# A threshold search on VectorE and ScalarE: part up to the threshold, a padding column, fewer pointer scalars

## The chip, the cores and the metric

One NeuronCore of a Trainium2 chip runs the whole program. Its engines are TensorE (PE; PEld is its weight load), VectorE (DVE), ScalarE (ACT), GpSimd (POOL) and SyncE (SP), each with an in-order queue; they wait for one another, and for DMAs, by semaphores. The metric is the device time of one execution in microseconds, given as the median of several runs; one further execution was profiled.

## The reference

Two graph layers over 3327 nodes with 256 features each, both with a residual and a layer norm in front. Nearly all of the change lies in the first one, which in each of two steps keeps, in every row of an attention matrix, the largest entries whose softmax mass reaches 0.9, and normalizes them again:

```python
def _adj_from_feats(Xa, W1, W2, W3):
    logits = (Xa @ W1) @ W2 @ (Xa @ W3).T / TAU
    idx = jnp.argsort(-logits, axis=1)
    vals = jnp.take_along_axis(logits, idx, axis=1)
    csum = jnp.cumsum(jax.nn.softmax(vals, axis=1), axis=1)
    k_i = jnp.sum(csum < P_NUC, axis=1) + 1          # P_NUC = 0.9
    keep_sorted = jnp.arange(logits.shape[1])[None, :] < k_i[:, None]
    keep = jnp.take_along_axis(keep_sorted, jnp.argsort(idx, axis=1), axis=1)
    return jax.nn.softmax(jnp.where(keep, logits, -jnp.inf), axis=1)

for s in range(2):
    A = _adj_from_feats(Xa, W1, W2, W3)
    Xf, Xb, Xa = Rf @ Xf, Rb @ Xb, A @ Xa
    Z = Z + (Xf @ U1[s] + Xb @ U2[s] + Xa @ U3[s])
```

The second layer is a masked softmax over x W (x W)^T with an edge mask, and a product with it.

## The kernel before, in words

The rows of the attention matrix are cut into 26 row tiles of 128 partitions; a row tile is 128 x 3327 in float32 (`rows`, six buffers of `NPAD` = 3328 columns, of which the last is zeroed once). Nothing is sorted. The exponentials x of a row are kept, with their sum Z, and a threshold `mid` is searched by 19 rounds of bisection on a logarithmic scale (`BISECT` = 19): each round asks whether the entries above `mid` hold 0.9 Z, and multiplies `mid` by one of two constants, `up` or `down` (`rate`). After 19 rounds `cut` zeroes what lies at or below `mid`, and its sum is the new normalizer.

`layer_step` is one of the two steps. Its row tiles run in nine triples g = 0 to 8. In triples 0 to 7 all three roles run side by side: VectorE searches the row tiles r = 0 and r = 1, ScalarE r = 2. This document calls such a triple a block. The last one, `LAST` = 8, has two row tiles: VectorE does r = 0 alone, ScalarE the first 10 rounds of r = 1 (`FIRST_PART`), then VectorE takes r = 1 over (`take_over`, `go_on`).

A round on VectorE is three instructions. `evaluate` (L720; `alone` L741 and `go_on` L758 in the last triple) is a pass over the row tile that sums x where x > `mid`; the accumulator read that ends it is an instruction of its own in the trace. `judge` (L727, L761) compares the sum with `target` = 0.9 Z, both on one column, and writes `hit`. `move` (L732, L764) sets `mid` = (`hit` + `down`) * `mid`. In a block the two row tiles alternate, one slot each, 38 slots in all: pass of r, `move` of the other one, `judge` of r, then `between`. `between` puts other work of VectorE into the slots by a table of beats (`due`): `take` (L699) evicts a 512-wide chunk of the next block's logits from PSUM, `highest` (L705) reduces their maxima, `cut` (L774), `scale`, `row_sums`, `row_rates`, `low_parts`. In the last triple each of the three waits for the one before.

A round on ScalarE has two passes over its row tile: Sign (L673), which counts, and Relu (L679), which sums what is above the threshold; `mid` is kept negated as a bias. `sides` prepares `base`, `fac` and `mean` from `mid`, `above` forms `over` from the count, `settle` the sign and the new `mid`. Between the passes and after the second, `fill` does ScalarE's other work by beats 0 to 39, two a round: it evacuates transposed weights from PSUM (`evacuate`, L552), for TensorE's products (`attend`), and outputs, issues DMAs, and takes the next block's three exponentials (L517) at beats 20, 29 and 37. TensorE's queue holds, beat by beat, the next logits (two PSUM banks, freed by `take`), transposes, `attend` and the sweeps of other products.

After the two steps come two phases, a middle one and one over the edges of the second layer.

Of the kernel before, what the change touches and what calls it, by code (L numbers as in the profile page):

```python
# [7 lines left out]
ALU = mybir.AluOpType  # L8
# [7 lines left out]
P = 128  # L16
# [323 lines left out]
def layer_step(nc, sem_in, psum, sb_in, s, qk, s_op, a_op, env):  # L340
# [40 lines left out]
    with ExitStack() as c:  # L381
        sb = sb_in(c)
        sem, cleared = sem_in(c)
        rows = sb(tag + "rows", [P, 6, NPAD], F32)
        dump = sb(tag + "dump", [P, N], BF16)
        adump = sb(tag + "adump", [P, N], I8)
# [6 lines left out]
            sb(tag + n, [P, 6], F32) for n in ("nb", "Z", "target", "mid", "hit", "mass", "kept", "rk"))  # L393
        cnt, gap, base, over, sgn, fac, mean = (sb(tag + n, [P, 1], F32) for n in ("cnt", "gap", "base", "over", "sgn", "fac", "mean"))
        u12 = sb(tag + "u12", [P, KC, 2 * D], F32)
        S = {n: sem(tag + n) for n in (
            "lg_done", "lg_free", "nb_ready", "exp_done", "w_ready", "rk_ready", "tr_done", "ev_done", "ax_done",
            "acc_free", "slab_used", "sa_free", "rows_zero", "a_eval", "a_begun", "a_base", "a_over", "a_sgn", "a_fac", "a_mid",
            "weights")}
# [31 lines left out]
        def row(g, r):  # L431
            return rows[:, home(g, r), 0:N]

        def w2d(ap):
# [78 lines left out]
        def _(act):  # L513
# [6 lines left out]
            def begin(g, r):  # L520
                act.wait_ge(S["exp_done"], LOADS.index((g, r)) + 1)
                nc.scalar.activation(st(target, g, 2), st(Z, g, r), ACT.Copy, scale=2.0 * P_NUC).then_inc(S["a_begun"], 1)
                nc.scalar.activation(st(mid, g, 2), st(Z, g, r), ACT.Copy, scale=-LEAST * 2.0 ** LOG_STEP).then_inc(S["a_begun"], 1)
                act.wait_ge(S["a_begun"], 2 * (g + 1))

            def sides(g, it):
                up, down = rate(it)
                last = -1.0 if it + 1 == BISECT else 1.0
                nc.scalar.activation(base[:], st(mid, g, 2), ACT.Identity, scale=float(N), bias=st(target, g, 2)).then_inc(S["a_base"], 1)
                nc.scalar.activation(fac[:], st(mid, g, 2), ACT.Copy, scale=last * (down - up) / 2).then_inc(S["a_fac"], 1)  # L530
                nc.scalar.activation(mean[:], st(mid, g, 2), ACT.Copy, scale=last * (down + up) / 2).then_inc(S["a_fac"], 1)

            def above(g, n):
                act.wait_ge(S["a_base"], n + 1)
                act.wait_ge(S["a_eval"], 2 * n + 1)
                nc.scalar.activation(over[:], cnt[:], ACT.Identity, scale=st(mid, g, 2), bias=base[:]).then_inc(S["a_over"], 1)

            def settle(g, n):
                act.wait_ge(S["a_over"], n + 1)
                act.wait_ge(S["a_eval"], 2 * n + 2)  # L540
                nc.scalar.activation(sgn[:], gap[:], ACT.Sign, scale=-2.0, bias=over[:]).then_inc(S["a_sgn"], 1)
                act.wait_ge(S["a_sgn"], n + 1)
                act.wait_ge(S["a_fac"], 2 * n + 2)
                nc.scalar.activation(st(mid, g, 2), sgn[:], ACT.Identity, scale=fac[:], bias=mean[:]).then_inc(S["a_mid"], 1)
                act.wait_ge(S["a_mid"], n + 1)

# [121 lines left out]
            for g in range(TRIPLES):  # L668
                r, rounds = (1, FIRST_PART) if g == LAST else (2, BISECT)
                begin(g, r)  # L670
                for it in range(rounds):
                    n = BISECT * g + it
                    nc.scalar.activation(adump[:], row(g, r), ACT.Sign, bias=st(mid, g, 2), accum_out=cnt[:]).then_inc(S["a_eval"], 1)  # L673
                    sides(g, it)
                    for b in beats(g, 2 * it):
                        fill(g, b)
                    above(g, n)
                    act.wait_ge(S["a_eval"], 2 * n + 1)
                    nc.scalar.activation(adump[:], row(g, r), ACT.Relu, bias=st(mid, g, 2), accum_out=gap[:]).then_inc(S["a_eval"], 1)  # L679
                    for b in beats(g, 2 * it + 1):  # L680
                        fill(g, b)
                    settle(g, n)
            for b in range(2 * FIRST_PART + NGRP + 4, 2 * BISECT):
# [6 lines left out]
        def _(dve):  # L690
# [16 lines left out]
            def begin(g, r):  # L707
                dve.wait_ge(S["exp_done"], LOADS.index((g, r)) + 1)
                nc.vector.tensor_scalar(st(target, g, r), st(Z, g, r), P_NUC, None, ALU.mult).then_inc(begun[r], 1)
                nc.vector.tensor_scalar(st(mid, g, r), st(Z, g, r), LEAST * 2.0 ** LOG_STEP, None, ALU.mult).then_inc(begun[r], 1)  # L710

            def evaluate(g, it, r):
                n = BISECT * g + it
                if it == 0:
                    dve.wait_ge(begun[r], 2 * (g + 1))
                else:
                    dve.wait_ge(mid_ready[r], n)
                if n + r >= 1:
                    dve.wait_ge(mass_done[1 - r], n + r)
                nc.vector.scalar_tensor_tensor(out=dump[:], in0=row(g, r), scalar=st(mid, g, r), in1=row(g, r),  # L720
                                               op0=ALU.is_gt, op1=ALU.mult, accum_out=st(mass, g, r)).then_inc(mass_done[r], 1)

            def judge(g, it, r):
                n = BISECT * g + it
                up, down = rate(it)
                dve.wait_ge(mass_done[r], n + 1)
                nc.vector.tensor_scalar(st(hit, g, r), st(mass, g, r), st(target, g, r), up - down, ALU.is_ge, ALU.mult).then_inc(hit_ready[r], 1)  # L727

            def move(g, it, r):
                n = BISECT * g + it  # L730
                dve.wait_ge(hit_ready[r], n + 1)
                nc.vector.tensor_scalar(st(mid, g, r), st(hit, g, r), rate(it)[1], st(mid, g, r), ALU.add, ALU.mult).then_inc(mid_ready[r], 1)  # L732

            def alone(it):
                n = BISECT * LAST + it
                if it == 0:
                    dve.wait_ge(begun[0], 2 * (LAST + 1))
                    dve.wait_ge(mass_done[1], n)
                else:
                    dve.wait_ge(mid_ready[0], n)  # L740
                nc.vector.scalar_tensor_tensor(out=dump[:], in0=row(LAST, 0), scalar=st(mid, LAST, 0), in1=row(LAST, 0),  # L741
                                               op0=ALU.is_gt, op1=ALU.mult, accum_out=st(mass, LAST, 0)).then_inc(mass_done[0], 1)
                judge(LAST, it, 0)
                move(LAST, it, 0)

            def take_over():
                dve.wait_ge(S["a_mid"], BISECT * LAST + FIRST_PART)
                nc.vector.tensor_scalar(st(target, LAST, 1), st(Z, LAST, 1), P_NUC, None, ALU.mult).then_inc(begun[1], 1)
                nc.vector.tensor_scalar(st(mid, LAST, 1), st(mid, LAST, 2), -1.0, None, ALU.mult).then_inc(mid_ready[1], 1)

            def go_on(it):
                n = BISECT * LAST + it - FIRST_PART
                up, down = rate(it)
                if it == FIRST_PART:
                    dve.wait_ge(begun[1], 2 * LAST + 1)
                    dve.wait_ge(mass_done[0], BISECT * TRIPLES)
                dve.wait_ge(mid_ready[1], n + 1)
                nc.vector.scalar_tensor_tensor(out=dump[:], in0=row(LAST, 1), scalar=st(mid, LAST, 1), in1=row(LAST, 1),  # L758
                                               op0=ALU.is_gt, op1=ALU.mult, accum_out=st(mass, LAST, 1)).then_inc(mass_done[1], 1)
                dve.wait_ge(mass_done[1], n + 1)  # L760
                nc.vector.tensor_scalar(st(hit, LAST, 1), st(mass, LAST, 1), st(target, LAST, 1), up - down,  # L761
                                        ALU.is_ge, ALU.mult).then_inc(hit_ready[1], 1)
                dve.wait_ge(hit_ready[1], n + 1)
                nc.vector.tensor_scalar(st(mid, LAST, 1), st(hit, LAST, 1), down, st(mid, LAST, 1), ALU.add, ALU.mult).then_inc(mid_ready[1], 1)  # L764

            def cut(g, r):
# [5 lines left out]
                else:  # L772
                    dve.wait_ge(mid_ready[r], BISECT * (g + 1))
                nc.vector.scalar_tensor_tensor(out=row(g, r), in0=row(g, r), scalar=st(mid, g, r), in1=row(g, r),  # L774
                                               op0=ALU.is_gt, op1=ALU.mult,
# [77 lines left out]
            for g in range(LAST):  # L853
                begin(g, 0)
                for it in range(BISECT):
                    for r in range(2):
# [3 lines left out]
                        if it + r >= 1:  # L860
                            move(g, it + r - 1, 1 - r)
                        judge(g, it, r)
                        between(g, 2 * it + r)
                cut(g, 0)
# [749 lines left out]
```

## Time and profile before

| | before |
|---|---|
| median of 3 runs | 3754.25 us (3752.21 to 3756.71) |
| profiled execution, own time | 3752.47 us |
| its span, first to last instruction | 3750.6 us |
| busy share DVE / ACT / PE / PEld / POOL | 94% / 84% / 78% / 55% / 10% |
| granted TensorE clock, mean | 0.892 |

The shares are of the whole span. A stretch's own busy times say which engine is full in it; the time of an instruction overlaps that of the next on the same engine, so two rows of the timeline are read by their starts. The idle time that a row names, and what ended it, belong to the engine in front of that instruction.

### The profile page before, as it was taken

How to read it: one execution, taken by the hardware profiler on the slowest of the kernel's cores; microseconds unless marked ns; L12 is line 12 of the kernel's file. 1: busy time of each engine (PE TensorE's matmuls, PEld its weight loads, DVE VectorE, ACT ScalarE, POOL GpSimd, SP SyncE). 2: the span in 40 equal slices, each digit the busy share in tenths (PEclk: the TensorE clock that was granted, in tenths of full speed). 3: DMA queues.
4: the chain of work that ended last, by engine and by line, in shares of the span. 5: the costliest groups of instructions: out<-in, count | busy, mean ns of one | idle time of the engine just before them, and what ended most of it. 6: DMA issues, size and time to landing. Idle time of an engine off the chain costs nothing. (4 is left out here: it accounts for less than half of the span.)

```text
span 3750.6 us, 42354 instructions
## 1 busy us (share of the span) xinstructions
PE 2934.6 (78%) x14004; PEld 2072.7 (55%) x14004; DVE 3507.9 (94%) x4688; ACT 3148.4 (84%) x4587; POOL 387.2 (10%) x457
## 2 busy tenths in 40 slices
PE   6568787787878788538879797978889754799998
PEld 4456666675757566413536354544536343567787
DVE  7999999999999999789999999999999995677887
ACT  6999999999999999479899999999999971344443
POOL 3000000000000000000000000000000002334444
PEclk9689888898989898769989898989999877999999
DMA  2112121312222220072121121212121103355563
GB/s 93 64 56 87 62 92 59 104 46 94 67 74 83 75 79 22 27 206 65 33 51 37 42 50 35 50 39 44 42 53 38 31 6 99 104 170 189 197 210 106
DMA packets 157020, 288.52 MB, mean 77 GB/s; under 512 B 14080, under 2 KB 93376, under 8 KB 153408
## 3 DMA queue, kind: packets, MB, share of 16 engines
q1 hardware_dynamic: 120400, 205.97, 17.7%
q10 hardware_dynamic: 21744, 62.79, 4.8%
q0 software_dynamic: 14656, 17.04, 3.3%
q8 instruction: 111, 1.82, 0.2%
q14 instruction: 109, 0.89, 0.1%
HBM read 232.80 MB, written 59.77 MB: 78 GB/s over the span
## 5 line engine op out<-in xcount | busy, mean ns | idle before, releaser
L720 DVE SCALAR_TENSOR_TENSOR s_dump<-s_rows,s_mid 128x3327 bf16<-128x3327 f32 x608 | 2238.5, 3682 | 2.3 <-issue 0.7
L673 ACT ACTIVATE s_adump<-s_rows,s_mid 128x3327 int8<-128x3327 f32 x324 | 995.1, 3071 | 10.5
L679 ACT ACTIVATE s_adump<-s_rows,s_mid 128x3327 int8<-128x3327 f32 x324 | 991.0, 3059 | 0.0
L932 PE MATMUL bank<-x,s_slab 128*128 128x512 f32 x1352 | 633.7, 612 | 0.0
L909 PE MATMUL bank<-kh,qs 128*128 128x512 f16 (+1 forms) x364 | 147.0, 404 | 379.6 <-DVE s_rows L699 369.5
L932 PEld LDWEIGHTS bank<-x,s_slab 128*128 128x128 f32 x1352 | 266.3, 198 | 280.3 <-issue 268.4
L976 PE MATMUL bank<-hb,s_wT 128*128 128x256 f32 x1352 | 358.4, 410 | 72.5 <-ACT s_wT L552 72.4
L976 PE MATMUL bank<-xab,s_wT 128*128 128x256 f32 x1352 | 349.1, 403 | 49.9 <-ACT s_wT L552 49.8
L965 PE MATMUL bank<-ident,s_rows 128*128 128x128 f32 x1352 | 231.3, 299 | 183.9 <-DVE s_rows L774 183.0
L932 PE MATMUL bank<-hb,s_slab 128*128 128x257 f32 x1352 | 351.0, 400 | 0.0
L976 PEld LDWEIGHTS bank<-hb,s_wT 128*128 128x128 f32 x1352 | 262.8, 205 | 123.1 <-ACT s_wT L552 55.9
L965 PEld LDWEIGHTS bank<-ident,s_rows 128*128 128x128 f32 x1352 | 188.5, 157 | 250.4 <-DVE s_rows L774 191.3
L976 PEld LDWEIGHTS bank<-xab,s_wT 128*128 128x128 f32 x1352 | 258.5, 202 | 93.0 <-ACT s_wT L552 42.3
L552 ACT ACTIVATE s_wT<-bank 128x512 f32<-128x512 f32 (+1 forms) x364 | 199.6, 550 | 127.9 <-PE bank L965 127.6
L909 PEld LDWEIGHTS bank<-kh,qs 128*128 128x128 f16 x364 | 42.9, 118 | 476.4 <-DVE s_rows L699 445.2
L932 PEld LDWEIGHTS bank<-hb,s_slab 128*128 128x128 f32 x1352 | 269.8, 202 | 60.2 <-issue 17.9
L1414 ACT ACTIVATE e_wh<-bank 128x512 f16<-128x512 f32 (+1 forms) x182 | 101.2, 565 | 202.0 <-PE bank L1546 201.6
L699 DVE TENSOR_SCALAR_CACHE_REDUCE s_rows<-bank 128x512 f32<-128x512 f32 (+1 forms) x364 | 232.7, 643 | 4.8 <-PE bank L910 3.4
L1363 POOL TENSOR_TENSOR e_rows<-e_rows,e_adj 128x3328 f32<-128x3328 f32 x25 | 181.2, 7247 | 233.2 <-ACT e_rows L1375 233.2
L937 PEld LDWEIGHTS bank<-hb,strip 128*128 128x128 f32 x1352 | 190.4, 197 | 13.2
L774 DVE SCALAR_TENSOR_TENSOR s_rows<-s_rows,s_mid 128x3327 f32<-128x3327 f32 x52 | 191.4, 3680 | 0.9
L494 POOL COPY qs<-s_q 64x128 f16<-64x128 f16 x26 | 32.5, 1249 | 1516.6 <-ACT s_q L618 1516.6
(183 smaller groups left out, 4824.2 us busy)
## 6 DMA issues: line engine op xcount, KB each, us to landing
s_slab<-adjT_dram SPq DMA_DIRECT2D x104, 448.0 KB, 3.9
s_slab<-adjT_dram SPq DMA_DIRECT2D x104, 384.0 KB, 3.7
e_adj<-adjR_dram ACTq DMA_DIRECT2D x23, 1664.0 KB, 7.2
strip<-adjR_dram SPq DMA_DIRECT2D x52, 448.0 KB, 3.5
strip<-adjR_dram SPq DMA_DIRECT2D x52, 384.0 KB, 3.3
e_ring<-sc_d SPq DMA_DIRECT2D x72, 256.0 KB, 5.4
sc_d<-e_stage SPq DMA_DIRECT2D x60, 256.0 KB, 2.4
su_d<-s_su_out ACTq DMA_DIRECT2D x26, 256.0 KB, 2.0
```

The source lines that it names most:

```text
L552: nc.scalar.activation(wT[:, n % 2, 0:w], bank_of("quad", n)[:, 0:w], ACT.Copy).then_inc(S["ev_done"], 1)
L673: nc.scalar.activation(adump[:], row(g, r), ACT.Sign, bias=st(mid, g, 2), accum_out=cnt[:]).then_inc(S["a_eval"], 1)
L679: nc.scalar.activation(adump[:], row(g, r), ACT.Relu, bias=st(mid, g, 2), accum_out=gap[:]).then_inc(S["a_eval"], 1)
L699: nc.vector.tensor_scalar(rows[:, home(g, r), ch * CH:ch * CH + w], psL[n % 2][:, 0:w], 1.0, None, ALU.mult, ALU.max, accum_out=mx[:, home ...
L720: nc.vector.scalar_tensor_tensor(out=dump[:], in0=row(g, r), scalar=st(mid, g, r), in1=row(g, r), op0=ALU.is_gt, op1=ALU.mult, accum_out=s ...
L774: nc.vector.scalar_tensor_tensor(out=row(g, r), in0=row(g, r), scalar=st(mid, g, r), in1=row(g, r), op0=ALU.is_gt, op1=ALU.mult, accum_out ...
L909: nc.tensor.matmul(psL[n % 2][:, 0:w], lhs, kh2[:, cols], start=True, stop=False)
L932: ins = nc.tensor.matmul(acc, slab[:, i % NSLAB, j - PIECES[p], :], s_op[:, j, 0:SN], start=False, stop=(j == NT - 1))
L937: ins = nc.tensor.matmul(psS[t % 2][:, SN + j:SN + j + 1], strip[:, i % 2, k * P:(k + 1) * P], s_op[:, 0, D:SN], start=False, stop=(j == N ...
L965: ins = nc.tensor.transpose(bank[:, k * P:(k + 1) * P], rows[:, home(g, r), j * P:(j + 1) * P], ident[:])
L976: ins = nc.tensor.matmul(psA[f % 2][:, 0:D], wT[:, n % 2, k * P:(k + 1) * P], a_op[:, j, 0:D], start=(j == 0), stop=(j == NT - 1))
L1363: nc.gpsimd.tensor_tensor(em[:, t % 3], em[:, t % 3], adj[:, t % 3], ALU.mult).then_inc(S["w_ready"], 1)
```

## The change

On VectorE the pass sums x where x <= `mid` instead of x > `mid`. It covers all 3328 columns (`wide_row`); `begin` writes (0.9 - 1) Z into the last one (`rest`) in place of `target`, so the sum is that of the entries up to `mid` less 0.1 Z, and `judge` compares it with the constant 0. `judge` then has two constants as scalars; `move` becomes a scalar_tensor_tensor with a constant as its scalar and `mid` as its second stream. `cut` covers the wide row too. `between` stands ahead of `judge`.

On ScalarE the second pass is Abs instead of Relu: with the sum of |x - t| and the count, `base` isn't needed, and its instruction goes. `target` becomes (2 * 0.9 - 1) Z. `above` and the second pass follow the first one directly; the even beat's `fill` moves behind the second pass, the odd one's behind `settle`. The wait for the new `mid` moves from the end of `settle` to the start of the next round.

```diff
-        dump = sb(tag + "dump", [P, N], BF16)
+        dump = sb(tag + "dump", [P, NPAD], BF16)
...
+        def wide_row(g, r):
+            return rows[:, home(g, r), :]
+
+        def rest(g, r):
+            return rows[:, home(g, r), N:NPAD]
...
             def sides(g, it):
...
-                nc.scalar.activation(base[:], st(mid, g, 2), ACT.Identity, scale=float(N), bias=st(target, g, 2)).then_inc(S["a_base"], 1)
...
             def above(g, n):
-                act.wait_ge(S["a_base"], n + 1)
                 act.wait_ge(S["a_eval"], 2 * n + 1)
-                nc.scalar.activation(over[:], cnt[:], ACT.Identity, scale=st(mid, g, 2), bias=base[:]).then_inc(S["a_over"], 1)
+                nc.scalar.activation(over[:], cnt[:], ACT.Identity, scale=st(mid, g, 2), bias=st(target, g, 2)).then_inc(S["a_over"], 1)
...
-                nc.scalar.activation(sgn[:], gap[:], ACT.Sign, scale=-2.0, bias=over[:]).then_inc(S["a_sgn"], 1)
+                nc.scalar.activation(sgn[:], gap[:], ACT.Sign, scale=-1.0, bias=over[:]).then_inc(S["a_sgn"], 1)
...
-                act.wait_ge(S["a_mid"], n + 1)
...
+                    if it >= 1:
+                        act.wait_ge(S["a_mid"], n)
                     nc.scalar.activation(adump[:], row(g, r), ACT.Sign, bias=st(mid, g, 2), accum_out=cnt[:]).then_inc(S["a_eval"], 1)
                     sides(g, it)
+                    above(g, n)
+                    nc.scalar.activation(adump[:], row(g, r), ACT.Abs, bias=st(mid, g, 2), accum_out=gap[:]).then_inc(S["a_eval"], 1)
                     for b in beats(g, 2 * it):
                         fill(g, b)
-                    above(g, n)
-                    act.wait_ge(S["a_eval"], 2 * n + 1)
-                    nc.scalar.activation(adump[:], row(g, r), ACT.Relu, bias=st(mid, g, 2), accum_out=gap[:]).then_inc(S["a_eval"], 1)
+                    settle(g, n)
                     for b in beats(g, 2 * it + 1):
                         fill(g, b)
-                    settle(g, n)
...
             def begin(g, r):
                 dve.wait_ge(S["exp_done"], LOADS.index((g, r)) + 1)
-                nc.vector.tensor_scalar(st(target, g, r), st(Z, g, r), P_NUC, None, ALU.mult).then_inc(begun[r], 1)
+                nc.vector.tensor_scalar(rest(g, r), st(Z, g, r), P_NUC - 1.0, None, ALU.mult).then_inc(begun[r], 1)
...
-                nc.vector.scalar_tensor_tensor(out=dump[:], in0=row(g, r), scalar=st(mid, g, r), in1=row(g, r),
-                                               op0=ALU.is_gt, op1=ALU.mult, accum_out=st(mass, g, r)).then_inc(mass_done[r], 1)
+                nc.vector.scalar_tensor_tensor(out=dump[:], in0=wide_row(g, r), scalar=st(mid, g, r), in1=wide_row(g, r),
+                                               op0=ALU.is_le, op1=ALU.mult, accum_out=st(mass, g, r)).then_inc(mass_done[r], 1)
...
-                nc.vector.tensor_scalar(st(hit, g, r), st(mass, g, r), st(target, g, r), up - down, ALU.is_ge, ALU.mult).then_inc(hit_ready[r], 1)
+                nc.vector.tensor_scalar(st(hit, g, r), st(mass, g, r), 0.0, up - down, ALU.is_le, ALU.mult).then_inc(hit_ready[r], 1)
...
-                nc.vector.tensor_scalar(st(mid, g, r), st(hit, g, r), rate(it)[1], st(mid, g, r), ALU.add, ALU.mult).then_inc(mid_ready[r], 1)
+                nc.vector.scalar_tensor_tensor(out=st(mid, g, r), in0=st(hit, g, r), scalar=rate(it)[1], in1=st(mid, g, r),
+                                               op0=ALU.add, op1=ALU.mult).then_inc(mid_ready[r], 1)
...
                         evaluate(g, it, r)
                         if it + r >= 1:
                             move(g, it + r - 1, 1 - r)
+                        between(g, 2 * it + r)
                         judge(g, it, r)
-                        between(g, 2 * it + r)
```

`alone`, `go_on`, `take_over` and `cut` are changed in the same way.

## Rows read from the trace of the kernel before

**Rows 1.** Stretches: length, busy us (instructions) of PE, PEld, DVE, ACT, POOL; clock, DMA.
```profile
581.90:754.80 172.90, 137.84 (x684) 110.92 (x684) 172.46 (x221) 168.34 (x247) 4.21 (x3) 0.88 0.24 76
3115.10:3750.60 635.50, 552.28 (x4198) 443.71 (x4198) 462.10 (x839) 266.61 (x432) 255.89 (x237) 0.96 0.49 159
```

**Rows 2.** VectorE's groups by line and shape: count, busy us, mean ns, idle before.
```profile
L720 DVE SCALAR_TENSOR_TENSOR s_dump<-s_rows,s_mid 128x3327 bf16<-128x3327 f32 x608 | 2238.5, 3682 | 2.3 <-issue 0.7
...
L732 DVE TENSOR_SCALAR s_mid<-s_hit,s_mid 128x1 f32<-128x1 f32 x646 | 135.2, 209 | 1.3
L727 DVE TENSOR_SCALAR s_hit<-s_mass,s_target 128x1 f32<-128x1 f32 x646 | 133.8, 207 | 1.9
...
L1187 DVE SCALAR_TENSOR_TENSOR m_x<-m_tin,m_inv 128x256 f32<-128x256 f32 x26 | 11.4, 478 | 0.0
...
L710 DVE TENSOR_SCALAR s_mid<-s_Z 128x1 f32<-128x1 f32 x34 | 4.9, 144 | 0.0
...
L1492 DVE TENSOR_TENSOR e_rows<-e_rows,e_adj 128x3328 f32<-128x3328 f32 x1 | 3.6, 3627 | 2.3 <-ACT e_rows L1375 2.3
```

**Rows 3.** Timeline of VectorE, steady slots: start us, length us, engine, line.
```profile
712.00 0.21 DVE L732 TENSOR_SCALAR s_mid<-s_hit,s_mid 128x1 f32<-128x1 f32 x1
712.13 0.21 DVE L727 TENSOR_SCALAR s_hit<-s_mass,s_target 128x1 f32<-128x1 f32 x1
712.25 0.68 DVE L699 TENSOR_SCALAR_CACHE_REDUCE s_rows<-bank 128x512 f32<-128x512 f32 x1
...
716.47 0.21 DVE L732 TENSOR_SCALAR s_mid<-s_hit,s_mid 128x1 f32<-128x1 f32 x1
716.59 0.21 DVE L727 TENSOR_SCALAR s_hit<-s_mass,s_target 128x1 f32<-128x1 f32 x1
716.72 3.68 DVE L720 SCALAR_TENSOR_TENSOR s_dump<-s_rows,s_mid 128x3327 bf16<-128x3327 f32 x1
```

**Rows 4.** Timeline of VectorE where a block begins.
```profile
758.61 0.08 DVE L720 DVE_READ_ACCUMULATOR s_dump<-s_rows,s_mid 128x1 f32 x1
758.72 0.21 DVE L727 TENSOR_SCALAR s_hit<-s_mass,s_target 128x1 f32<-128x1 f32 x1
758.85 0.14 DVE L709 TENSOR_SCALAR s_target<-s_Z 128x1 f32<-128x1 f32 x1
758.91 0.14 DVE L710 TENSOR_SCALAR s_mid<-s_Z 128x1 f32<-128x1 f32 x1
759.09 3.69 DVE L720 SCALAR_TENSOR_TENSOR s_dump<-s_rows,s_mid 128x3327 bf16<-128x3327 f32 x1
```

**Rows 5.** Timeline of VectorE in the last triple of step 1.
```profile
2988.93 0.21 DVE L727 TENSOR_SCALAR s_hit<-s_mass,s_target 128x1 f32<-128x1 f32 x1
2989.18 0.21 DVE L732 TENSOR_SCALAR s_mid<-s_hit,s_mid 128x1 f32<-128x1 f32 x1
2989.43 3.69 DVE L741 SCALAR_TENSOR_TENSOR s_dump<-s_rows,s_mid 128x3327 bf16<-128x3327 f32 x1
```

**Rows 6.** ScalarE: three groups by line, then two rows of its timeline.
```profile
L679 ACT ACTIVATE s_adump<-s_rows,s_mid 128x3327 int8<-128x3327 f32 x324 | 991.0, 3059 | 0.0
...
L529 ACT ACTIVATE s_base<-s_mid,s_target 128x1 f32<-128x1 f32 x324 | 90.5, 279 | 0.0
...
L265 ACT ACT_TABLE_LOAD x1 | 1.3, 1283 | 0.7 <-PEq L1607 0.7
...
732.77 0.28 ACT L529 ACTIVATE s_base<-s_mid,s_target 128x1 f32<-128x1 f32 x1
732.95 0.19 ACT L530 ACTIVATE s_fac<-s_mid 128x1 f32<-128x1 f32 x1
```

**Rows 7.** Timeline of ScalarE: the third exponential for the block that begins at 754.75.
```profile
745.39 3.06 ACT L517 ACTIVATE s_rows<-s_rows,s_nb 128x3327 f32<-128x3327 f32 x1
```

**Rows 8.** Timeline of VectorE: the take-over in step 0, with idle time before.
```profile
1531.49 0.15 DVE L748 TENSOR_SCALAR s_target<-s_Z 128x1 f32<-128x1 f32 x1 [0.97 <-ACT s_mid L544]
```

**Rows 9.** Waits from 409 to 1273 us: total us, times, longest us.
```profile
PE bank L909 <- DVE s_rows L699: 91.2, 36, 6.0
```

More of the change, by code:

```diff
@@ L393, in layer_step @@
             sb(tag + n, [P, 6], F32) for n in ("nb", "Z", "target", "mid", "hit", "mass", "kept", "rk"))
-        cnt, gap, base, over, sgn, fac, mean = (sb(tag + n, [P, 1], F32) for n in ("cnt", "gap", "base", "over", "sgn", "fac", "mean"))
+        cnt, gap, over, sgn, fac, mean = (sb(tag + n, [P, 1], F32) for n in ("cnt", "gap", "over", "sgn", "fac", "mean"))
         u12 = sb(tag + "u12", [P, KC, 2 * D], F32)
@@ L397, in layer_step @@
             "lg_done", "lg_free", "nb_ready", "exp_done", "w_ready", "rk_ready", "tr_done", "ev_done", "ax_done",
-            "acc_free", "slab_used", "sa_free", "rows_zero", "a_eval", "a_begun", "a_base", "a_over", "a_sgn", "a_fac", "a_mid",
+            "acc_free", "slab_used", "sa_free", "rows_zero", "a_eval", "a_begun", "a_over", "a_sgn", "a_fac", "a_mid",
             "weights")}
@@ L521, in begin @@
                 act.wait_ge(S["exp_done"], LOADS.index((g, r)) + 1)
-                nc.scalar.activation(st(target, g, 2), st(Z, g, r), ACT.Copy, scale=2.0 * P_NUC).then_inc(S["a_begun"], 1)
+                nc.scalar.activation(st(target, g, 2), st(Z, g, r), ACT.Copy, scale=2.0 * P_NUC - 1.0).then_inc(S["a_begun"], 1)
                 nc.scalar.activation(st(mid, g, 2), st(Z, g, r), ACT.Copy, scale=-LEAST * 2.0 ** LOG_STEP).then_inc(S["a_begun"], 1)
@@ L740, in alone @@
                     dve.wait_ge(mid_ready[0], n)
-                nc.vector.scalar_tensor_tensor(out=dump[:], in0=row(LAST, 0), scalar=st(mid, LAST, 0), in1=row(LAST, 0),
-                                               op0=ALU.is_gt, op1=ALU.mult, accum_out=st(mass, LAST, 0)).then_inc(mass_done[0], 1)
+                nc.vector.scalar_tensor_tensor(out=dump[:], in0=wide_row(LAST, 0), scalar=st(mid, LAST, 0), in1=wide_row(LAST, 0),
+                                               op0=ALU.is_le, op1=ALU.mult, accum_out=st(mass, LAST, 0)).then_inc(mass_done[0], 1)
                 judge(LAST, it, 0)
@@ L747, in take_over @@
                 dve.wait_ge(S["a_mid"], BISECT * LAST + FIRST_PART)
-                nc.vector.tensor_scalar(st(target, LAST, 1), st(Z, LAST, 1), P_NUC, None, ALU.mult).then_inc(begun[1], 1)
+                nc.vector.tensor_scalar(rest(LAST, 1), st(Z, LAST, 1), P_NUC - 1.0, None, ALU.mult).then_inc(begun[1], 1)
                 nc.vector.tensor_scalar(st(mid, LAST, 1), st(mid, LAST, 2), -1.0, None, ALU.mult).then_inc(mid_ready[1], 1)
@@ L757, in go_on @@
                 dve.wait_ge(mid_ready[1], n + 1)
-                nc.vector.scalar_tensor_tensor(out=dump[:], in0=row(LAST, 1), scalar=st(mid, LAST, 1), in1=row(LAST, 1),
-                                               op0=ALU.is_gt, op1=ALU.mult, accum_out=st(mass, LAST, 1)).then_inc(mass_done[1], 1)
+                nc.vector.scalar_tensor_tensor(out=dump[:], in0=wide_row(LAST, 1), scalar=st(mid, LAST, 1), in1=wide_row(LAST, 1),
+                                               op0=ALU.is_le, op1=ALU.mult, accum_out=st(mass, LAST, 1)).then_inc(mass_done[1], 1)
                 dve.wait_ge(mass_done[1], n + 1)
-                nc.vector.tensor_scalar(st(hit, LAST, 1), st(mass, LAST, 1), st(target, LAST, 1), up - down,
-                                        ALU.is_ge, ALU.mult).then_inc(hit_ready[1], 1)
+                nc.vector.tensor_scalar(st(hit, LAST, 1), st(mass, LAST, 1), 0.0, up - down, ALU.is_le, ALU.mult).then_inc(hit_ready[1], 1)
                 dve.wait_ge(hit_ready[1], n + 1)
-                nc.vector.tensor_scalar(st(mid, LAST, 1), st(hit, LAST, 1), down, st(mid, LAST, 1), ALU.add, ALU.mult).then_inc(mid_ready[1], 1)
+                nc.vector.scalar_tensor_tensor(out=st(mid, LAST, 1), in0=st(hit, LAST, 1), scalar=down, in1=st(mid, LAST, 1),
+                                               op0=ALU.add, op1=ALU.mult).then_inc(mid_ready[1], 1)
             def cut(g, r):
@@ L773, in cut @@
                     dve.wait_ge(mid_ready[r], BISECT * (g + 1))
-                nc.vector.scalar_tensor_tensor(out=row(g, r), in0=row(g, r), scalar=st(mid, g, r), in1=row(g, r),
+                nc.vector.scalar_tensor_tensor(out=wide_row(g, r), in0=wide_row(g, r), scalar=st(mid, g, r), in1=wide_row(g, r),
                                                op0=ALU.is_gt, op1=ALU.mult,
```

## The prediction

> **What bounds the kernel now.** The first view to read is the busy time by stretch. From 582 to 755 us, one block of three row tiles of the search, VectorE is busy 172.46 of 172.90 us, while ScalarE has about 4.6 us to spare and TensorE 35; the last 635.5 us belong to phases that the diff doesn't touch [rows 1]. There are 16 such blocks (eight in each of two layer steps), and two short ones that end a step. So VectorE's chain of instructions sets the time of the search, 16 x 172.9 us = 2766 us and the two short blocks, and what it sheds there the kernel sheds, until ScalarE or TensorE comes late. The second view is the groups by line: a search pass costs 3682 ns, and each of 646 rounds also has a `judge` (207 ns) and a `move` (209 ns) on one column [rows 2]. The third is the timeline, because durations overlap: what counts is the distance from one start to the next. In a slot with an eviction, `move` starts at 712.00, `judge` at 712.13, the eviction at 712.25. In a slot with nothing between, `move` starts at 716.47, `judge` at 716.59 and the next pass at 716.72 [rows 3]. Either small instruction thus holds VectorE for 0.125 us, 0.25 us together, and ends some 82 ns after its follower began.
>
> **`judge` without a pointer.** Where both scalars are constants, one column takes 0.14 us, and the next instruction starts 0.06 us later (758.85 to 758.91) [rows 4]. I take 0.062 instead of 0.125 us. One limit stays: what reads a pass's sum starts 0.11 to 0.12 us after the accumulator read (758.61 to 758.72) [rows 4]. The old `move` filled that time; a shorter one leaves part of it open.
>
> **`move` as scalar_tensor_tensor with a constant.** This form is not in the trace. With a pointer, the form costs 3682 ns at 3327 columns and 478 at 256 [rows 2]: 1.043 ns a column and 212 ns for a single one. A tensor_tensor, also two streams and without a pointer, takes 3627 ns at 3328 columns [rows 2], so some 156 for one. Taking the price of a pointer (207 against 144, 64 ns) off 212 gives 148. I take 152, near both, and so 0.070 us of engine time. The ends are 144 (as cheap as the constant-only form: 0.062) and 212 (the constant saves nothing: 0.130). Below or above these I see no reason. Something that waits for its result starts 0.04 us after its end: a constant-only writer is followed at 0.18 (758.91 to 759.09), a pointer one at 0.25 (2989.18 to 2989.43) [rows 4, 5]. For the new `move` that is 0.19 us (ends 0.18 and 0.25).
>
> The Trainium skill's VectorE: DVE Perf Modes, section "The TRN2 errata", gives an SBUF instruction 58 cycles plus its columns at 0.96 GHz, whatever its scalars; worked out from it, an estimate of 61 ns for one column, and nothing to gain: the kernel would stay at 3753 us, against 3685 by the rows. The rows at 0.125 against 0.06 us speak against that for pointers, and agree for constants [rows 3, 4].
>
> **The sum, by slots.** By `between`'s beats the 16 blocks of 38 slots have 401 with work between (evictions, maxima, cuts, low parts), 175 without, 16 first slots (no `move`), and 16 last ones, with a cut behind.
> - With work between: before 0.25. After, `move` 0.070, the work, then `judge` 0.062; the sum has long been there, which is what the new order of `between` and `judge` is good for. 0.118 each, 401 times: 47.3 us.
> - Without work, and last slots: the next pass waits for the `move` in front of the `judge`, 0.19 us after its start; `judge` (start at 0.12, held 0.062) ends at about the same time. 0.25 becomes 0.19: 0.060, 191 times: 11.5 us.
> - First slots: `judge` alone, 0.063, 16 times: 1.0 us. The `move` ahead of a block's second cut: 0.055, 16 times: 0.9 us.
> - The two short blocks run one row tile at a time, 19 + 9 rounds each: pass, `judge`, `move`, each waiting for the one before at 0.25 us (2988.93, 2989.18, 2989.43) [rows 5]. The two become 0.18 and 0.19: 0.128, 56 times: 7.2 us.
> - Against it: the wide pass and the wide cut have one column more, 1.04 ns, on 664 passes and 52 cuts: 0.7 us. `begin` and `take_over` issue as many instructions as before.
>
> Together 67.9 less 0.7 is 67.2 us. With the cheapest `move` it is 72.9, with the dearest 27.4.
>
> **ScalarE.** The round loses the base instruction: 279 ns long, 0.18 us to the next start (732.77 to 732.95) [rows 6]. 19 of them are 3.5 us a block, 60 us in all, none on the path as long as VectorE bounds. VectorE sheds about (67.2 - 7.2) / 16 = 3.8 us a block, so ScalarE must not lose more than its 4.6 us of idle and the missing 0.3 us. The even beats' evacuations go behind the second pass, where they cover the wait for its sum; the odd ones go behind the new threshold and cover part of that wait, where they covered the other one before. I cost this between 0 and 1 us a block, in either direction. Cover stays: the third exponential starts at 745.39 and lasts 3.06 us [rows 7], and the row tile that needs it first begins at 758.85 [rows 4], ten microseconds after. A lag of 0.5 us a block over eight blocks would fit in. Where the cover is thin is the end of step 0: VectorE waits 0.97 us for ScalarE's tenth round [rows 8]. There VectorE sheds 19 x 0.128 = 2.4 us and ScalarE 10 x 0.18 = 1.8, so this wait may be 0 to 2 us instead of 1. I cost it at no change.
>
> **What is moved.** The even evacuations come later by a pass (3059 ns long [rows 6]), and TensorE's products behind them too. Its queue holds the next logits behind these products, and VectorE's evictions wait for the logits. TensorE has two banks of lead: in five blocks it waited 91.2 us in 36 waits, up to 6.0 us, for evictions to free them [rows 9]. A shift of 3 us fits. ScalarE's DMA issues move with their beats; the stores they make are needed in the next step only. SP's queue loads slabs as TensorE's sweeps free them; these slip by the same 3 us, with two or three slabs loaded ahead. POOL adds ScalarE's outputs in DRAM, and ScalarE needs their buffers again a row tile later, a third of a block.
>
> So the forecast is 3752.47 us (the profiled execution's own time, 1.9 us more than its span) less 67.2, **3685.3 us**, say 3685. The runs' median, 3754.25, lies 1.8 us above this profile; the range holds that.
>
> **Rivals.**
> - The constant in the two-stream form saves nothing: `move` keeps its price, 27.4 us are saved, 3725 us. For it: no row has the form. Against it: tensor_tensor, at 156, has two streams and no pointer [rows 2]. Chance 0.06.
> - The waits in empty slots don't bind, and all 191 save 0.118: 11 us more, 3674 us. Against it: 0.18 and 0.25 behind a writer [rows 4, 5]. Chance 0.04.
> - The small instructions' start-to-start time is the sequencer's and not the pointer's, so that nothing is saved: 3752.5 + 0.7 = 3753 us. Against it: 0.06 against 0.125 in neighbouring rows [rows 4]. Chance 0.03. (This is what the errata section quoted above comes to.)
> - Slower, by TensorE: its lead is less than the pass by which the even evacuations slip. Then in the two even beats that have both an evacuation and an eviction (10 and 12), logits come 3.3 us late: 2 x 3.3 x 16 = 106 us lost, 3752.5 - 67.2 + 106 = 3791 us. It decides from a lead under about 3 us; the waits of up to 6.0 us speak against it [rows 9]. Chance 0.03.
> - Slower, by ScalarE: Abs is not in the function table that is loaded once, 1283 ns, in the whole span [rows 6]. Then each round switches twice, 19 x 2 x 1.283 = 48.8 us a block; ScalarE, with 172.9 - 4.6 - 3.5 = 164.8 of its own, needs 213.6 where a block lasted 172.9: 40.7 us more, 16 times, some 4400 us. It decides as soon as switching costs over 4 us a block. Exp, Sign, Relu, Identity and Copy share the one load, which says nothing of Abs. Chance 0.02.
>
> The Trainium skill's ScalarE: Activation LUTs, section "Table sets", says that abs is filler in every set; by that no load is added and this last rival falls. No run here has shown it.
>
> **How the numbers follow.** The forecast has 0.80; 0.02 is left for a ScalarE that falls behind by more than its cover, within some 20 us. About 0.2%, 7.5 us, is what a measurement of this kernel can tell from no change. Faster: 0.80 + 0.06 + 0.04 + 0.02 = 0.92; same 0.03; slower 0.05. The range runs from 3673 (empty slots save in full) to 3712 (a `move` of some 190 ns, or a ScalarE that is late by 20 us and more).
>
> **What would show it.** `judge` falls from 207 to about 145 ns and `move` from 209 to about 152. In an empty slot the distance from accumulator read to next pass falls from 0.25 to 0.19; with an eviction, `move` is followed at 0.07. A block falls from 172.9 to about 169 us, with VectorE still idle for well under 1 us in it and ScalarE idle for some microseconds. There is one table load. The forecast is wrong if idle time of VectorE appears ahead of evictions, exponentials' readers or the first cut of a block, or if `move` is at 209 or above.

## The result and the profile after

| | before | after |
|---|---|---|
| median | 3753.57 us (4 runs) | 3730.95 us (4 runs, 3729.09 to 3731.34) |
| ratio | 1 | 0.9937, 95% interval 0.9923 to 0.9952 |
| profiled execution, its span | 3752.47, 3750.6 us | 3731.06, 3729.3 us |
| busy DVE, whole span | 3507.9 us | 3446.5 us |

The change saves 22.6 us, a third of the 67.2 that were forecast, and the time lies outside the range (3673 to 3712). VectorE's busy time fell by 61.4 us, so most of the forecast work did go; 40 us of it came back as idle time. The stretches tell where. Each row has the columns of [rows 1]; the first is a block, the next two run from the begin of the last triple to its last cut, in step 0 and step 1, and the two behind them are the same stretches of the kernel before:

```profile
572.50:741.80 169.30, 139.15 (x684) 110.97 (x684) 168.81 (x219) 161.96 (x228) 1.80 (x3) 0.89 0.24 78
1415.20:1564.20 149.00, 98.39 (x392) 73.14 (x392) 123.92 (x139) 91.41 (x143) 3.52 (x4) 0.81 0.05 18
2954.10:3090.30 136.20, 69.59 (x304) 57.54 (x304) 120.15 (x127) 81.22 (x115) 5.11 (x6) 0.76 0.06 6
```
```profile
1441.80:1573.10 131.30, 90.72 (x391) 67.39 (x389) 127.05 (x139) 93.88 (x151) 4.19 (x4) 0.84 0.06 21
2985.00:3111.30 126.30, 61.81 (x301) 51.60 (x299) 123.19 (x126) 85.11 (x127) 5.11 (x6) 0.77 0.06 7
```

The block is down from 172.90 to 169.30 us with VectorE full, as argued; ScalarE has 7.3 us to spare in it instead of 4.6 [rows 1]. The last triples, 131.3 and 126.3 us long before, have grown to 149.0 and 136.2, and VectorE is idle in them for 25.1 and 16.1 us, where it was for 4.3 and 3.1. From the first begin to the last triple's, the eight blocks went from 1371.7 to 1344.3 us in step 0 and from 1363.3 to 1340.8 in step 1: -27.4 and -22.5, while VectorE's busy time in them fell by 27.4 and 28.1. With +17.7 and +9.9 in the last triples that is -22.3 of the span's -21.3. What comes after the last cut of a step is as long as before, within a microsecond.

VectorE's groups of the two small instructions, which answer to [rows 2]:

```profile
L736 DVE SCALAR_TENSOR_TENSOR s_mid<-s_hit,s_mid 128x1 f32<-128x1 f32 x646 | 101.4, 157 | 1.3
L731 DVE TENSOR_SCALAR s_hit<-s_mass 128x1 f32<-128x1 f32 x646 | 96.8, 150 | 2.5
```

`judge` is down from 207 to 150 ns, `move` from 209 to 157, close to the 145 and 152 that were said. The wide pass costs nothing that shows (3679 ns on average against 3682). The timeline of an empty slot and of one with an eviction, as [rows 3]:

```profile
627.91 0.15 DVE L736 SCALAR_TENSOR_TENSOR s_mid<-s_hit,s_mid 128x1 f32<-128x1 f32 x1
628.02 0.15 DVE L731 TENSOR_SCALAR s_hit<-s_mass 128x1 f32<-128x1 f32 x1
628.10 3.69 DVE L724 SCALAR_TENSOR_TENSOR s_dump<-s_rows,s_mid 128x3328 bf16<-128x3328 f32 x1
...
631.71 0.16 DVE L736 SCALAR_TENSOR_TENSOR s_mid<-s_hit,s_mid 128x1 f32<-128x1 f32 x1
631.78 0.69 DVE L703 TENSOR_SCALAR_CACHE_REDUCE s_rows<-bank 128x512 f32<-128x512 f32 x1
...
632.39 0.15 DVE L731 TENSOR_SCALAR s_hit<-s_mass 128x1 f32<-128x1 f32 x1
632.46 3.68 DVE L724 SCALAR_TENSOR_TENSOR s_dump<-s_rows,s_mid 128x3328 bf16<-128x3328 f32 x1
```

The empty slot spends 0.19 us on the two (627.91 to 628.10), the other one 0.07 and 0.07. Both are the forecast's.

What VectorE waits for now, in total us, times, longest us, and behind it `low_parts` in the kernel before:

```profile
DVE kl L803 <- ACT s_q L621: 38.8, 3, 23.7
...
DVE s_rows L753 <- ACT s_mid L548: 19.8, 2, 12.9
...
DVE s_rows L703 <- PE bank L915: 8.9, 18, 2.5
```
```profile
DVE kl L798 <- ACT s_q L618: 23.4, 1, 23.4
```

The take-over (L753) waits 19.8 us for ScalarE's tenth round; before, it waited 0.97 us in step 0 [rows 8] and nothing in step 1. `low_parts` (L803) waits 15.1 us in the last triple of step 0; before, its one wait, 23.4 us, lay behind the last cut of that step, and a wait as long (23.7) lies there still. Evictions (L703) wait 8.9 us for logits against 3.4; the 5.4 us that are new lie in the blocks of step 1, and none in those of step 0. The first two are the last triples.

ScalarE's timeline at the start of the last triple of step 0 shows why:

```profile
1416.30 0.57 ACT L555 ACTIVATE s_wT<-bank 128x512 f32<-128x512 f32 x1
1416.77 0.28 ACT L545 ACTIVATE s_sgn<-s_gap,s_over 128x1 f32<-128x1 f32 x1
1417.09 0.39 ACT L548 ACTIVATE s_mid<-s_sgn,s_mean,s_fac 128x1 f32<-128x1 f32 x1
1417.38 0.57 ACT L555 ACTIVATE s_wT<-bank 128x512 f32<-128x512 f32 x1
1421.60 0.60 ACT L555 ACTIVATE s_wT<-bank 128x512 f32<-128x512 f32 x1 [3.64 <-PE bank L970]
...
1428.99 1.08 ACT L555 ACTIVATE s_wT<-bank 128x512 f32<-128x512 f32 x2
1429.95 0.31 ACT L545 ACTIVATE s_sgn<-s_gap,s_over 128x1 f32<-128x1 f32 x1
1430.29 0.39 ACT L548 ACTIVATE s_mid<-s_sgn,s_mean,s_fac 128x1 f32<-128x1 f32 x1
1434.31 0.60 ACT L555 ACTIVATE s_wT<-bank 128x512 f32<-128x512 f32 x1 [3.64 <-PE bank L970]
1436.69 0.38 ACT L555 ACTIVATE s_wT<-bank 128x256 f32<-128x256 f32 x1 [1.78 <-PE bank L970]
```

In the last triple `beats` gives each half of a round two beats, hence two evacuations in the first rounds, where a block has one. Before, a pass stood between one pair and the next, and TensorE did its products meanwhile. Now both pairs come one after the other (1428.99, then 1434.31 and 1436.69), with only the two small settling instructions between. There are two `wT` buffers and two banks, so the third evacuation has to wait until TensorE has used the first and transposed the next piece (up to four 128 x 128 tiles) into its bank, and ScalarE stands still. Then it runs two passes in a row, and TensorE stands still. ScalarE's evacuations in its ten rounds of step 0 and step 1, with the idle time before them and what ended most of it, the first two now, the next two in the kernel before:

```profile
L555 ACT ACTIVATE s_wT<-bank 128x512 f32<-128x512 f32 (+1 forms) x21 | 11.3, 558 | 22.4 <-PE bank L970 22.4
L555 ACT ACTIVATE s_wT<-bank 128x512 f32<-128x512 f32 (+1 forms) x22 | 11.9, 558 | 21.1 <-PE bank L970 21.1
```
```profile
L552 ACT ACTIVATE s_wT<-bank 128x512 f32<-128x512 f32 (+1 forms) x21 | 11.2, 553 | 3.3 <-PE bank L965 3.2
L552 ACT ACTIVATE s_wT<-bank 128x512 f32<-128x512 f32 (+1 forms) x21 | 11.2, 553 | 7.5 <-PE bank L965 7.4
```

### The profile page after: what moved, and what is told of

Same layout as the page of the kernel before. It is cut to its first block and busy times, and to the rows that moved or that the text cites. A ratio compares the mean times of both kernels' runs of the same rounds, so it can differ in the third digit from the quotient of the medians.

```text
span 3729.3 us, 41687 instructions
## 1 busy us (share of the span) xinstructions
PE 2935.2 (79%) x14004; PEld 2079.7 (56%) x14004; DVE 3446.5 (92%) x4688; ACT 3067.7 (82%) x4263; POOL 387.3 (10%) x457
## 3 DMA queue, kind: packets, MB, share of 16 engines
q1 hardware_dynamic: 120400, 205.97, 17.7%
## 5 line engine op out<-in xcount | busy, mean ns | idle before, releaser
L724 DVE SCALAR_TENSOR_TENSOR s_dump<-s_rows,s_mid 128x3328 bf16<-128x3328 f32 x608 | 2236.8, 3679 | 2.1 <-issue 0.9
L937 PE MATMUL bank<-x,s_slab 128*128 128x512 f32 x1352 | 624.5, 605 | 0.0
L981 PE MATMUL bank<-xab,s_wT 128*128 128x256 f32 x1352 | 360.7, 413 | 89.1 <-ACT s_wT L555 88.8
L981 PEld LDWEIGHTS bank<-xab,s_wT 128*128 128x128 f32 x1352 | 266.0, 207 | 136.5 <-ACT s_wT L555 60.4
L703 DVE TENSOR_SCALAR_CACHE_REDUCE s_rows<-bank 128x512 f32<-128x512 f32 (+1 forms) x364 | 233.8, 646 | 10.4 <-PE bank L915 8.9
L779 DVE SCALAR_TENSOR_TENSOR s_rows<-s_rows,s_mid 128x3328 f32<-128x3328 f32 x52 | 191.4, 3682 | 0.7
```

The source lines that it names most:

```text
L703: nc.vector.tensor_scalar(rows[:, home(g, r), ch * CH:ch * CH + w], psL[n % 2][:, 0:w], 1.0, None, ALU.mult, ALU.max, accum_out=mx[:, home ...
L724: nc.vector.scalar_tensor_tensor(out=dump[:], in0=wide_row(g, r), scalar=st(mid, g, r), in1=wide_row(g, r), op0=ALU.is_le, op1=ALU.mult, a ...
L779: nc.vector.scalar_tensor_tensor(out=wide_row(g, r), in0=wide_row(g, r), scalar=st(mid, g, r), in1=wide_row(g, r), op0=ALU.is_gt, op1=ALU. ...
L937: ins = nc.tensor.matmul(acc, slab[:, i % NSLAB, j - PIECES[p], :], s_op[:, j, 0:SN], start=False, stop=(j == NT - 1))
L981: ins = nc.tensor.matmul(psA[f % 2][:, 0:D], wT[:, n % 2, k * P:(k + 1) * P], a_op[:, j, 0:D], start=(j == 0), stop=(j == NT - 1))
```

## The experiments

Seven kernels. The times are medians of four runs each (ten for the row of four), the ratios against the kernel before on the same chip (3754.73 us for the first four, 3754.09 for the others).

**The last triple back to its old places.** The changed kernel, with ScalarE's other work where it was, for the last triple alone:

```diff
                     sides(g, it)
+                    early = g == LAST
+                    if early:
+                        for b in beats(g, 2 * it):
+                            fill(g, b)
                     above(g, n)
                     nc.scalar.activation(adump[:], row(g, r), ACT.Abs, ...)
-                    for b in beats(g, 2 * it):
+                    for b in beats(g, 2 * it + 1 if early else 2 * it):
                         fill(g, b)
                     settle(g, n)
-                    for b in beats(g, 2 * it + 1):
-                        fill(g, b)
+                    if not early:
+                        for b in beats(g, 2 * it + 1):
+                            fill(g, b)
```

> The changed kernel, with the other work of ScalarE put back to its old places in the last triple alone (even beat between the two passes, odd beat between the second pass and the sign); base stays removed. Theory A: in the last triple each half of a round has two evacuations, the new places put four in a row, and the third and fourth wait for TensorE (22.4 and 21.1 us of such waits in the last triple of step 0 and 1, against 3.3 and 7.5 before), which makes VectorE wait at the take-over and at its low parts. Then these waits fall to under 8 us a step, VectorE's stretch from the begin of the last triple to its last cut falls from 149.0 and 136.2 us to about 129 and 124, and the time is some 3699 us. Theory B: the waits come from VectorE reaching the take-over earlier, whatever ScalarE's places: then 3725 us or more.

Measured: 3700.0 us, ratio 0.9855 (0.984 to 0.987), 31 us less than the changed kernel. The two last triples, then ScalarE's evacuations in its ten rounds of each:

```profile
1415.10:1543.30 128.20, 85.58 (x389) 63.55 (x388) 123.94 (x140) 91.43 (x142) 7.01 (x4) 0.86 0.06 21
2935.60:3058.80 123.20, 58.90 (x301) 49.24 (x299) 120.09 (x127) 83.45 (x118) 5.11 (x6) 0.78 0.06 7
```
```profile
L555 ACT ACTIVATE s_wT<-bank 128x512 f32<-128x512 f32 (+1 forms) x21 | 11.3, 555 | 1.8 <-PE bank L975 1.7
L555 ACT ACTIVATE s_wT<-bank 128x512 f32<-128x512 f32 (+1 forms) x21 | 11.2, 555 | 2.4 <-PE bank L975 2.2
```

128.2 and 123.2 us, as theory A has it, and 1.7 and 2.2 us of waits for TensorE instead of 22.4 and 21.1. Theory B falls: VectorE reaches the take-over of step 0 earlier than in the changed kernel, where `low_parts` had held it up, and waits 1.1 us there.

**VectorE's half alone.** ScalarE's code is that of before, `base` included.

> VectorE's half of the change alone: ScalarE has its base instruction, Relu, and the old places. Theory A: the blocks last about 169.3 and 167 us as in the changed kernel, the last triples have few waits on TensorE (3 to 8 us), VectorE waits about 3 us at the take-over of step 0 (0.97 plus 19 x 0.128); 3697 to 3705 us. Theory B: VectorE waits 7 us or more at both take-overs; 3725 us or more. A third possibility: ScalarE with its base instruction is the bound of the blocks; then these last over 170 us and VectorE is idle in them.

Measured: 3702.74 us, ratio 0.9863 (0.9848 to 0.9877). The waits of VectorE in question:

```profile
DVE s_rows L705 <- PE bank L917: 11.9, 20, 2.2
DVE s_rows L755 <- ACT s_mid L550: 5.2, 1, 5.2
```

A single wait at a take-over, as theory A has it, but 5.2 us and not 3. New are 11.9 us of waits for logits, more than in any other kernel, and the blocks of step 1 take 1344.0 us together against 1334.9 with the old places and no base (below). I read this as a trace of the third possibility: with its base instruction ScalarE is slower, TensorE waits for its evacuations, and the logits stand behind those in TensorE's queue. The traces show the middle of it: in the blocks of step 1 TensorE waits 65.0 us for evacuations here and 43.0 us there. That the logits come late for this reason is argued.

**ScalarE's half alone.** VectorE's code is that of before; the moved work and the missing base stay.

> ScalarE's half of the change alone: VectorE has its pointer scalars and the old sum. Theory A: blocks unchanged at 172.7 and 170.4 us, waits on TensorE in the last triples at about 20 us as in the changed kernel, VectorE waits at low parts and the take-over; slower than before by 15 to 30 us, some 3775 us. Theory B: as before within 5 us, 3750 to 3755 us.

Measured: 3779.76 us, ratio 1.0066 (1.0051 to 1.0081): this half makes the kernel slower by 25.0 us. The waits of VectorE, and ScalarE's evacuations in its ten rounds of step 0:

```profile
DVE kl L796 <- ACT s_q L615: 36.2, 2, 23.4
DVE s_target L746 <- ACT s_mid L542: 15.8, 2, 9.0
```
```profile
L549 ACT ACTIVATE s_wT<-bank 128x512 f32<-128x512 f32 (+1 forms) x21 | 11.3, 558 | 22.8 <-PE bank L963 22.8
```

ScalarE's waits are those of the changed kernel (22.8 us against 22.4) without any edit on VectorE: its speed has no part in them. In the blocks the missing base saves nothing, as VectorE sets their length (172.9 us, as before).

**The old places everywhere.** `early = True` in the first experiment's code; base stays removed, Abs stays.

> The changed kernel with the old places of ScalarE's other work in all triples (base removed, Abs). Theory A: the last triples as with the old places there alone; the blocks at 169 and 167 us or a little less, since evacuations are not a pass late and VectorE's waits for logits (8.9 us against 3.4 before) go back; 3690 to 3700 us. If the new places are what keeps ScalarE in pace in the blocks, these grow instead and VectorE waits for exponentials: over 3710 us.

Measured: 3692.46 us, ratio 0.9834 (0.9818 to 0.985), the fastest of all these kernels, 38.5 us faster than the changed one. The last triples last 128.3 and 123.2 us. VectorE's waits for logits:

```profile
DVE s_rows L708 <- PE bank L920: 3.2, 13, 0.7
```

Against the first experiment the last triples are the same, and so are the blocks of step 0 (1344.4 us in both); the other 7.5 us are the blocks of step 1 (1334.9 us against 1342.5), and 6.8 of them the evictions' waits (10.0 us there). So ScalarE's work that comes a pass late does reach VectorE in those blocks too, by way of TensorE's logits, though by little. Against VectorE's half alone, 10.3 us are what the lighter ScalarE round (no base, Abs for Relu) brings once its other work is left in place.

**Judge ahead of the work between.** On the old places everywhere:

```diff
                         if it + r >= 1:
                             move(g, it + r - 1, 1 - r)
-                        between(g, 2 * it + r)
                         judge(g, it, r)
+                        between(g, 2 * it + r)
```

> Against the changed kernel with the old places of ScalarE's work everywhere (3692.5 us): judge ahead of the work between again. If a judge directly behind a 0.072 us move waits for the pass's sum until 0.118 us after the accumulator read, a slot with work between costs 0.118 + 0.066 instead of 0.072 + 0.066 us: 0.046 more, 401 times, 18 us; some 3711 us, blocks about 1.1 us longer. If the sum is there in time and the order is worth nothing: 3691 to 3695 us.

Measured: 3716.09 us, ratio 0.9899 (0.9883 to 0.9916), 23.6 us more. A slot with an eviction:

```profile
636.05 0.15 DVE L741 SCALAR_TENSOR_TENSOR s_mid<-s_hit,s_mid 128x1 f32<-128x1 f32 x1
636.16 0.15 DVE L736 TENSOR_SCALAR s_hit<-s_mass 128x1 f32<-128x1 f32 x1
636.23 0.68 DVE L708 TENSOR_SCALAR_CACHE_REDUCE s_rows<-bank 128x512 f32<-128x512 f32 x1
```

The judge stands 0.11 us behind the move, waiting for the sum, and 0.18 us go by before the eviction starts. With a cheap `move` the order of `between` and `judge` is worth 23.6 us. 18 were expected.

**Four evacuations in a row, but early.** On the old places everywhere; in the last triple both beats of a round stand between the two passes:

```diff
+                    both = g == LAST
+                    for h in (2 * it, 2 * it + 1) if both else (2 * it,):
+                        for b in beats(g, h):
+                            fill(g, b)
                     above(g, n)
                     nc.scalar.activation(adump[:], row(g, r), ACT.Abs, ...)
+                    if not both:
+                        for b in beats(g, 2 * it + 1):
+                            fill(g, b)
                     settle(g, n)
```

> The old places everywhere (3692.5 us), but in the last triple both beats of a round, four evacuations, between the two passes: in a row, yet earlier than before. If it is the row of four that makes ScalarE wait for TensorE, the waits in the last triples are again 15 to 25 us each, VectorE waits at low parts and the take-over, and the time is 3710 to 3735 us. If it is that the work comes a pass later, there are none of these waits, and the time is 3692 us or a little less.

Measured: 3746.36 us, ratio 0.9978 (0.9969 to 0.9988), 53.9 us more, above the range that was expected for the row. ScalarE's evacuations in its ten rounds of step 0 and step 1, and VectorE's wait at the take-overs:

```profile
L555 ACT ACTIVATE s_wT<-bank 128x512 f32<-128x512 f32 (+1 forms) x21 | 11.3, 556 | 24.4 <-PE bank L973 24.3
L555 ACT ACTIVATE s_wT<-bank 128x512 f32<-128x512 f32 (+1 forms) x22 | 11.9, 559 | 30.4 <-PE bank L973 30.4
```
```profile
DVE s_rows L756 <- ACT s_mid L548: 36.2, 2, 23.1
```

A row of four is enough to bring the waits, without any work being late: nothing here is later than with the old places. Whether the lateness adds to them in the changed kernel is not shown. Why the row costs more here than in the changed kernel was not tried; there the two pairs have at least the settling instructions between them.

**Move with its pointer again.** On the old places everywhere, `move` and `go_on` with the old tensor_scalar:

```diff
-                nc.vector.scalar_tensor_tensor(out=st(mid, g, r), in0=st(hit, g, r), scalar=rate(it)[1], in1=st(mid, g, r),
-                                               op0=ALU.add, op1=ALU.mult).then_inc(mid_ready[r], 1)
+                nc.vector.tensor_scalar(st(mid, g, r), st(hit, g, r), rate(it)[1], st(mid, g, r), ALU.add, ALU.mult).then_inc(mid_ready[r], 1)
```

> The old places everywhere (3692.5 us), but move again as tensor_scalar with a pointer; judge with constants. By the slots: 0.054 x 401 + 0.052 x 191 + 0.057 x 56 + 0.06 x 16 = 36 us more, some 3728 us, with move at 209 ns and 0.126 us from start to start. If VectorE's small instructions are partly covered: under 15 us more.

Measured: 3723.85 us, ratio 0.992 (0.9905 to 0.9935), 31.4 us more, where 36 were expected.

```profile
L741 DVE TENSOR_SCALAR s_mid<-s_hit,s_mid 128x1 f32<-128x1 f32 x646 | 135.1, 209 | 1.3
```

The form of one instruction on one column, run 646 times, is worth 0.9% of the kernel. The edit changes the form and the pointer together, so the pointer's own part is not shown here; `judge`, which kept its form, shows it (207 ns with the pointer, 150 without).

## Why the prediction was wrong

- **What bounds the kernel**: right. In the blocks VectorE is full before and after. In step 0 they fell by what VectorE shed (27.4 us), in step 1 by 22.5 of 28.1. (The 16 blocks last 2735.0 us together before; 16 x 172.9 takes the longer ones of step 0 for all.)
- **`judge` and `move`**: right within 5 ns each (150 and 157 ns against 145 and 152). The form that the trace before didn't have lay between the two ends that were given, 144 and 212 ns, and next to the 156 of the tensor_tensor.
- **The sum by slots**: right in its mechanism, 5 us too large. The kernel with the old places everywhere, which has all of VectorE's edits and none of the new waits, saves 62.3 us where 67.2 were said. A slot with work spends 0.07 + 0.07 us, where 0.070 + 0.062 were said, and an empty one 0.19 (627.91 to 628.10 above) to 0.21, where 0.19 was: some 0.01 us more than the terms, over 592 slots. That `judge` must stand behind the work between was right too: 23.6 us.
- **ScalarE in the blocks**: right. It kept pace; its lead was not used up. Removing its base is not free of effect: 10.3 us, where nothing was counted. In the traces VectorE's waits for logits (11.9 and 3.2 us) and at the take-over (5.2 and 1.1 us) differ with it.
- **The end of a step: the step that failed.** "so this wait may be 0 to 2 us instead of 1. I cost it at no change." It was 19.8 us at the two take-overs and 15.1 at `low_parts`. The working counted ScalarE's own instructions (10 x 0.18 us) and not what its moved work waits for. It also took the last triple to be like a block, whereas `beats` doubles the work there: two evacuations a half-round. Four in a row outrun two buffers. The two last triples together came out 27.6 us longer where 7.2 less were forecast: 34.8 us. Undoing the places there alone took 33.8 us out of the two triples and 31.0 off the time, and a row of four put elsewhere brought the waits back. By the spans 45.9 us of the forecast are missing: these 34.8, then 10.1 in the blocks (4.5 that VectorE did not shed, and 5.6 of idle time in step 1), and 1.0 elsewhere.
- **What is moved: "A shift of 3 us fits"**: nearly. It holds in step 0; in the blocks of step 1 evictions wait 5.4 us, where they didn't wait before. With the old places everywhere these are gone (3.2 us of such waits in the whole span, 3.4 before the change), and the kernel is 7.5 us faster than with the last triples mended alone. The rival on TensorE had the mechanism, at far too large a price (106 us): its lead of two banks takes up most of the shift.
- **Rivals**: the dear `move` (3725), the empty slots without a wait (3674) and small instructions that save nothing (3753) fall by the timeline and by the last experiment. A pointer costs 57 ns in `judge`; `move` shed 52 ns with its pointer, but its form changed too. The Trainium skill's VectorE: DVE Perf Modes, section "The TRN2 errata", has a formula without a term for a pointer; the measurement differs and decides. There is one table load, 1283 ns, as before, with Abs among the functions, so the dear Abs falls too. The Trainium skill's ScalarE: Activation LUTs, section "Table sets", has abs in every set; this trace agrees.

The range missed because it had some 20 us for a ScalarE that falls behind in the blocks, but 2 us at most for the wait at the end of a step, without a bound from the rows on TensorE's time between two evacuations. Before, ScalarE already stood up to 1.69 us between the two evacuations of a pair in that triple.

## What to carry to other kernels

When work is moved within an engine's queue, count not only its own instructions. Ask what another engine did for it while the long instruction between two pieces ran. If the pieces are put next to each other and there are more of them than buffers, that other engine's time shows in full. Look for the stretches where the schedule is denser than in the steady state, such as the last group, and cost those by their own rows. And of two halves of a change measure each alone: here one was worth 52 us and the other cost 25.

## What the runs showed of the hardware

TensorE ran slower after it had stood still. Its timeline in the changed kernel, and its clock in two stretches of 4 us (the last figure but two of each row):

```profile
1423.56 1.89 PE L981 MATMUL bank<-hb,s_wT 128*128 128x256 f32 x8
...
1429.64 3.78 PE L981 MATMUL bank<-hb,s_wT 128*128 128x256 f32 x8 [3.75 <-ACT s_wT L555]
```
```profile
1422.00:1426.00 4.00, 3.89 (x22) 3.18 (x21) 3.90 (x5) 4.00 (x9) 0.00 (x0) 1.00 0.01 4
...
1430.00:1434.00 4.00, 4.00 (x12) 3.17 (x12) 4.00 (x6) 0.64 (x3) 0.00 (x0) 0.50 0.00 0
```

After 3.75 us of idle time while ScalarE ran its passes, the granted clock was 0.50, the lower of the two levels (1.2 GHz), and eight products took 3.78 us; at 1.00 (2.4 GHz) they took 1.89. In the next three rounds eight products took 2.78, 3.15 and 3.28 us behind idle times of 4.13, 3.39 and 4.25 us. ScalarE's wait for the third evacuation, 3.64 us, lies over the slow products and the transposes behind them. Over the whole last triples the clock was 0.81 and 0.76, against 0.84 and 0.77 before (rows of the result). No run held the clock, so how much of the 35 us is its doing stays open.

A pointer scalar on one column costs VectorE 57 ns of length in `judge` (207 against 150 ns), and about as much from start to start (0.125 us against 0.07).
